# Second attention: a unit's last two batches of key tiles become one batch of four, with six buffers of exponentials

## What is computed

```python
mask = (q_idx >= k_idx) & (q_idx - k_idx <= WINDOW)      # WINDOW = 1024
scores = jnp.einsum('bhqd,bhkd->bhqk', q, k) / np.sqrt(HD)   # 16 heads of 32
attn = jax.nn.softmax(jnp.where(mask, scores, NEG), axis=-1)
out = jnp.einsum('bhqk,bhkd->bhqd', attn, v)
```

## Time and profile before

| | |
|---|---|
| median of 3 runs | 1531.86 us (1527.9 to 1532.23) |
| profiled execution, own time | 1528.64 us |
| its span, first to last instruction | 1526.9 us |
| mean granted TensorE clock | 0.984 |
| PE busy | 1463.1 us, 96% |
| DVE, ACT, POOL busy | 1027.9, 755.3, 464.2 us |
| S, line 2022 | 576 matmuls, 135.9 us |
| V, line 2059 | 1152 matmuls, 221.3 us |
| M, line 2000 | 592 matmuls, 179.0 us |

### The profile page before, as it was taken

The page is one execution under the profiler, slowest core; times in us unless marked ns, Lnnn a source line. Parts: engine busy times, 40 slices in busy tenths (PEclk is TensorE's granted clock), DMA queues, the critical chain, the costliest instruction groups (busy, mean ns, idle before and its releaser), DMA issues. The chain is left out here.

```text
span 1526.9 us, 23551 instructions
## 1 busy us (share of the span) xinstructions
PE 1463.1 (96%) x6981; PEld 1060.2 (69%) x6981; DVE 1027.9 (67%) x2940; ACT 755.3 (49%) x1282; POOL 464.2 (30%) x697
## 2 busy tenths in 40 slices
PE   6999999999999999999989999999999997998997
PEld 4778788888777888788855555555555554787776
DVE  6453666666658647887768886665668985678592
ACT  5633555656564535433325555555555553235561
POOL 0000577777620113323221212222212214053062
PEclk9999999999999999999969999999999999999999
DMA  5001222221100434466696405325145028743121
GB/s 187 1 1 45 108 90 76 86 103 76 56 29 26 146 102 121 138 195 192 191 241 281 112 16 121 71 59 122 28 100 121 6 81 259 208 173 138 31 81 14
DMA packets 106932, 161.53 MB, mean 106 GB/s; under 512 B 12640, under 2 KB 63728, under 8 KB 100432
## 3 DMA queue, kind: packets, MB, share of 16 engines
q1 hardware_dynamic: 101292, 152.53, 33.0%
q10 hardware_dynamic: 4516, 5.38, 1.0%
q0 software_dynamic: 1024, 2.43, 0.8%
HBM read 117.44 MB, written 42.87 MB: 105 GB/s over the span
## 5 line engine op out<-in xcount | busy, mean ns | idle before, releaser
L2147 ACT ACTIVATE l_pt<-banks 128x1024 f32<-128x1024 f32 (+3 forms) x288 | 218.6, 811 | 137.2 <-PE banks L2022 135.2
L2219 DVE CUSTOM_DVE_ANT_0 stage<-banks,l_edges 128x384 f32<-128x384 f32 (+3 forms) x384 | 201.8, 542 | 72.8 <-issue 71.5
L2059 PE MATMUL banks<-l_pt,l_v 128*64 128x512 f32 (+3 forms) x1152 | 221.3, 505 | 0.3 <-POOL l_pt L2117 0.3
L718 POOL TENSOR_TENSOR ex_hl<-ex_h,ex_hh 128x512 fp32r<-128x512 f32 x128 | 165.6, 1300 | 81.2 <-ACT ex_hh L686 81.0
L2116 POOL TENSOR_TENSOR l_turn<-l_before 128x2 f32<-128x2 f32 x192 | 38.9, 203 | 382.7 <-ACT l_pt L2147 373.3
L751 DVE SCALAR_TENSOR_TENSOR ex_rw<-banks,ex_wb 128x512 f32<-128x512 f32 x128 | 88.3, 691 | 78.9 <-PE banks L75 78.8
L2222 DVE TENSOR_REDUCE l_mx<-banks 128x1 f32<-128x384 f32 (+1 forms) x208 | 113.1, 544 | 39.8 <-PE banks L2000 39.0
L686 ACT ACTIVATE ex_hh<-ex_h 128x512 fp32r<-128x512 f32 x128 | 80.9, 632 | 103.5 <-DVE ex_h L759 102.0
L2059 PEld LDWEIGHTS banks<-l_pt,l_v 128*64 128x64 f32 x1152 | 69.1, 137 | 89.3 <-issue 67.8
L73 PE MATMUL banks<-ex_xlh,ex_wh 128*128 128x512 f32 x256 | 101.7, 397 | 2.0 <-DVE ex_rw L751 2.0
L74 PE MATMUL banks<-ex_xll,ex_wh 128*128 128x512 f32 x256 | 99.8, 390 | 0.0
(11 more groups left out here) (458 smaller groups left out, 3488.4 us busy)
## 6 DMA issues: line engine op xcount, KB each, us to landing
ex_wb<-gates_by_expert SPq DMA_DIRECT2D x16, 1024.0 KB, 4.7
l_v<-layer_v SPq DMA_DIRECT2D x8, 1024.0 KB, 17.2
layer_qk<-qkv_yh SPq DMA_DIRECT2D x30, 256.0 KB, 3.2
layer_qk<-qkv_yl SPq DMA_DIRECT2D x30, 256.0 KB, 3.6
layer_v<-qkv_vs SPq DMA_DIRECT2D x15, 512.0 KB, 4.6
ex_ws<-ew_in SPq DMA_DIRECT2D x16, 384.0 KB, 4.9
l_q<-layer_qk SPq DMA_DIRECT2D x12, 512.0 KB, 7.7
l_k<-layer_qk SPq DMA_DIRECT2D x12, 512.0 KB, 13.3
```

Of the source, the lines that this page charges most:

```text
L718: pool.tensor_tensor(hl[:, k % RING, :], h[:, k % RING, :], raw(hh[:, k % RING, :]), ALU.subtract).then_inc(hl_done, 1)
L2059: last = pe.matmul(bank[h * 2 * HD:(h + 1) * 2 * HD, (qa - b * BT) * P:(qz + 1 - b * BT) * P], v[par][:, kt, h, :], pt[:, step_part(b, j), ...
L2147: act.activation(pt[:, step_part(b, j), :, 0:width], G.banks[:, 2 * slot:2 * slot + 2, 0:width], ACT.Exp, scale=scale).then_inc(p_done, 1)
L2219: dve.tensor_tensor_reduce(cutoff[:, n % 4, 0:width], G.ps[5 + n % MB][:, 0:width], masked, 1.0, NEG, ALU.add, ALU.max, mx[:, h, m, c:c + ...
```

## The change

The last two batches of every unit become one batch of four key tiles (`BATCHES`). In such a batch at j the order of PE is: two places of the stream, S(j + 2), one place, S(j + 3), all the other places that the two batches had, S of the next unit's first two key tiles, then V of j, j + 1, j + 2 and j + 3 together. In the very last unit `picks` stands where the next unit's S would. Blocks 1 to 3 keep their batches of two before it; block 0, with four key tiles, is a batch of four alone. Batches of two keep their order.

Six buffers of exponentials replace four: four where they were, two in a new tile `far`. To make room, `junk` (a result of the ranking that nobody reads) has one half instead of two, and the one-hot tile moves to the place of the first value tile, free by then. ACT's first `output` also waits for the last writes of the stage before (`v_out`, `qk_out`).

```diff
-    PR = 4
+    PR, NEAR = 6, 4
+    BATCHES = [[4], [2, 2, 4], [2, 2, 2, 2, 4], [2, 2, 2, 2, 4]]
+        far = M.sb("far", [P, PR - NEAR, 2, TB])
...
-            return (keys_before[b] + j) % PR
+            n = (keys_before[b] + j) % PR
+            return pt[:, n, :, :] if n < NEAR else far[:, n - NEAR, :, :]
...
-                    for j in range(0, steps, 2):
-                        events = list(due(i, position(u, j + 1), last))
-                        ahead = min(MB, len(events)) if j + 2 < steps else len(events)
-                        for at in events[:ahead]:
-                            maximum(*at)
+                    for j, size in zip(accumulate([0] + BATCHES[b][:-1]), BATCHES[b]):
+                        events = [at for n in range(1, size, 2) for at in due(i, position(u, j + n), last)]
...
+                        else:
+                            for n, part in ((2, events[:2]), (3, events[2:MB])):
+                                for at in part:
+                                    maximum(*at)
+                                scores(i, u, j + n)
+                            for at in events[MB:]:
+                                maximum(*at)
+                            if end:
+                                picks()
+                            else:
+                                scores(i, u + 1, 0)
+                                scores(i, u + 1, 1)
+                        for n in range(size):
+                            values(i, u, j + n)
...
+                if not i_at_least(i, u, 1):
+                    for n in range(2):
+                        act.wait_ge(G.v_out[n], 16 * NT // 2)
+                        act.wait_ge(G.qk_out[n], 64 * NT // 2)
                 act.activation(ob[:, b % 2, :], G.ps[4], ACT.Copy).then_inc(o_sb, 1)
```

More of the change, by code:

```diff
@@ L11 @@
 from contextlib import ExitStack
+from itertools import accumulate
 import numpy as np
@@ L1793, in stage_attend1 @@
         "sr_in", "iota", "link", "sel", "pos_mm", "oh", "pick_mm"))
-    PR = 4
+    PR, NEAR = 6, 4
     LEAD = 37
-    PLACES, PICKS = 0, 8
+    BATCHES = [[4], [2, 2, 4], [2, 2, 2, 2, 4], [2, 2, 2, 2, 4]]
+    PLACES = 0
     MB = 3
@@ L1807, in stage_attend1 @@
         wraw = nc.alloc_sbuf_tensor_at("l1_wraw", [P, NC, D], F32, offset=v0_at)
-        pt = nc.alloc_sbuf_tensor_at("l1_pt", [P, PR, 2, TB], F32, offset=G.qw_at)
+        pt = nc.alloc_sbuf_tensor_at("l1_pt", [P, NEAR, 2, TB], F32, offset=G.qw_at)
         ob = M.sb("ob", [P, 2, TB])
         dn, dn2 = M.sb("dn", [P, 2 * H0 * TB // P]), M.sb("dn2", [P, H0 * TB // P])
-        sr, junk, same = G.out_o1[:, :, :].rearrange("p g n -> p (g n)"), M.sb("junk", [P, 2, T], BF16), M.sb("same", [P, 2, P])
+        sr, junk, same = G.out_o1[:, :, :].rearrange("p g n -> p (g n)"), M.sb("junk", [P, T], BF16), M.sb("same", [P, 2, P])
         count, rank_of, sel = M.sb("count", [P, NT, 6]), M.sb("rank", [P, NT]), M.sb("sel", [P, NT], BF16)
@@ L1814, in stage_attend1 @@
         order, before = M.sb("order", [P, SEL]), M.sb("before", [P, P])
-        onehot, number = junk[:, :, :].rearrange("p a (b n) -> p (a b) n", n=SEL), M.sb("number", [P, NT, 2], BF16)
+        onehot, number = nc.alloc_sbuf_tensor_at("l1_onehot", [P, NT, SEL], BF16, offset=v0_at), M.sb("number", [P, NT, 2], BF16)
         onesb, parti = M.sb("onesb", [P, P], BF16), M.sb("parti", [P, NT], I32)
@@ L2059, in values @@
                     last = pe.matmul(bank[h * 2 * HD:(h + 1) * 2 * HD, (qa - b * BT) * P:(qz + 1 - b * BT) * P],
-                                     v[par][:, kt, h, :], pt[:, step_part(b, j), h, 0:(qz - qa + 1) * P],
+                                     v[par][:, kt, h, :], step_part(b, j)[:, h, 0:(qz - qa + 1) * P],
                                      start=j == 0, stop=j == len(plans[b].keys) - 1)
@@ L2072, in body @@
                     end = last and u == 2 * NB - 1
-                    steps = len(plans[b].keys)
-                    for j in range(0, steps, 2):
-                        events = list(due(i, position(u, j + 1), last))
-                        ahead = min(MB, len(events)) if j + 2 < steps else len(events)
-                        for at in events[:ahead]:
-                            maximum(*at)
+                    assert sum(BATCHES[b]) == len(plans[b].keys)
+                    for j, size in zip(accumulate([0] + BATCHES[b][:-1]), BATCHES[b]):
+                        events = [at for n in range(1, size, 2) for at in due(i, position(u, j + n), last)]
                         if end and j == PLACES:
                             places()
[L2081 to L2091, removed]
+                        if size == 2:
+                            for at in events[:MB]:
+                                maximum(*at)
+                            scores(i, u, j + 2)
+                            scores(i, u, j + 3)
+                            for at in events[MB:]:
[3 more added lines that the diff above has]
+                                for at in part:
+                                    maximum(*at)
+                                scores(i, u, j + n)
+                            for at in events[MB:]:
+                                maximum(*at)
+                            if end:
[5 more added lines that the diff above has]
+                            values(i, u, j + n)
             looped(pe, PAIRS // 2, body)
@@ L2112, in masked @@
                 at, sign = (0, 1) if cut(b, j) == "diag" else ((qz - qa) * P, -1)
-                tile = pt[:, step_part(b, j), :, at:at + P]
+                tile = step_part(b, j)[:, :, at:at + P]
                 pool.wait_ge(p_done, keys + j + 1)
@@ L2146, in exponentials @@
                 wait(act, av_mm, n - PR + 1)
-                act.activation(pt[:, step_part(b, j), :, 0:width],
+                act.activation(step_part(b, j)[:, :, 0:width],
                                G.banks[:, 2 * slot:2 * slot + 2, 0:width], ACT.Exp, scale=scale).then_inc(p_done, 1)
@@ L2257, in rank @@
                     k0, k1 = pieces[n]
-                    dve.tensor_scalar(junk[:, t % 2, k0:k1], sr[:, k0:k1], own, 0.0, ALU.is_ge if k1 <= t * P else ALU.is_gt,
+                    dve.tensor_scalar(junk[:, k0:k1], sr[:, k0:k1], own, 0.0, ALU.is_ge if k1 <= t * P else ALU.is_gt,
                                       ALU.add, accum_out=count[:, t, n:n + 1])
```

## The result

The changed kernel takes 1543.29 us (median of 4 runs, 1540.88 to 1543.76) against 1532.05 us of the kernel before: 1.008 times as long, with a 95% interval of 1.0068 to 1.0092. The medians differ by 11.2 us. The forecast was 1545, between 1539 and 1552, and slower; the time lies inside. The profiled execution took 1543.76 us, against 1528.64 before: 15.1 us more, where the sum said 15. These two executions are further apart than the medians, since the one of before lies 3.4 us under its kernel's median and the one of after 0.5 above.

What follows compares the result with a forecast made beforehand. PE was taken to set the time, and merged batches to wait for banks held by DVE and ACT. Pairs' costs, saved V blocks included, summed to +15 us: 1545 forecast, range 1539 to 1552, 8 in 10 between 1534 and 1564.

Steps and rivals of the forecast that it cites:

- The bank rule: In merged batches, M needs a bank DVE has reduced, one each 0.475 us: place n + 3 not before 1.11 + 0.475 (n - 1).
- Block 0: Last batches' first place to next unit's first: from 6.04 to 6.53 us, +0.5, with PE waiting 1.2 us for banks.
- ACT's copies: Block 1's merged batch: seventh place waits for ACT's two copies until 2.91 us, next S until 3.5; stretch 6.83, +0.8.
- The V block's worth: One V block less in each of 32 units saves 0.35 us, between 0.155 and 0.465: -11.2 us in all.
- Block 3: Stretch with R second of five places: ACT's copies done at 1.94 us, S at 2.4, end at 4.8 against 4.23, +0.55.
- Block 2: Stretch with five narrow M and no R: 4.1 us against 3.97, +0.1.
- The first unit of the stage: Pair 0, block 0: three reductions no longer run under V0 and V1, +1.4 us, less 0.35 for the V block.
- Pair 7: Last pair, stream run out by blocks 2 and 3: 0.5, 0.8, 0 and -0.3 us for the four blocks, 1.0 together.
- What costs nothing: Six buffers, POOL's masks, ACT's `output` and new wait, `junk` and the one-hot tile add no time; `picks` within 0.4 us.
- rival 2: The clock also falls after the new waits, about 1.5 us a fall: 1557, or 1569 with blocks 0 and 1; chance 0.16.
- The sum: Whole program: pairs 1 to 6 11.7 us, pair 0 2.5, pair 7 1.0; +15 us on the profiled 1528.64, 1543.6.
- Rival 1: Drains go and no wait comes, if DVE returns a bank each 0.2 us, not 0.475: 1519 us; chance 0.10.

Runs made afterwards that it cites:

- e_short_after: The changed kernel with each of DVE's reductions cut to 128 columns of a bank: 1516.68 us, 0.9908 of the kernel before.
- e_buffers: All of the change but the batches of four, against the kernel before (six buffers, batches of two in the old order): 1531.25 us, ratio 1.0008.
- e_blocks01: The changed kernel with the batch of four in blocks 0 and 1 only, batches of two in blocks 2 and 3: 1544.75 us, 1.0102 of the kernel before.
- e_short_before: The kernel before with each of DVE's reductions cut to 128 columns of a bank: 1506.58 us, 0.9851 of the kernel before.
- LEAD = 41 and 44: Changed kernel, stream lead 41 or 44 for 37, stream places in batches of four split around the next unit's S: 1536.19 and 1535.61 us.

## Why the prediction was right

Most steps held and a few did not. The waits inside the merged batches are the ones that I named, in the places that I named.

- **The bank rule.** M behind the second narrow S spaced by 0.475: measured 0.47 to 0.49. V block of 4, 3, 2, 1 at 2.31: measured 2.30. Block 0 came out 0.09 above the forecast, block 2 0.04. e_short_after shows the cause, by taking it away.
- **ACT's copies.** Last bank at 2.91 behind the batch's start: the M released by them came 2.89 behind it (998.48 to 1001.37). The next unit's first S I had at 3.5, it came at 3.59, and S then took 1.12 (1002.07 to 1003.19) in place of 1.01: the first S after a wait takes 0.34 to the second, where 0.23 is usual. I had kept such a surcharge (0.1 for the weights behind each M that waited) for the upper bound, and should have put it into the sum wherever a wait stands right ahead. Block 3 (+0.70 for +0.55) has a like surplus, 0.06 ahead of S and 0.09 in it.
- **The V block's worth.** 0.35 (0.36 by its own terms), between 0.155 and 0.465. Where little wait is left, 0.27 (block 0, short reductions); with reductions of full length and spread places 0.18. The value taken was somewhat high; the rest of it, two thirds of M's and S's surplus (0.31), was an estimate, and about half of it is there.
- **Block 2** I had from pairs of odd number alone. In even ones the third narrow S of before starts 0.33 behind the second (953.41 to 953.74), twice the 0.16 between the first two; after the change an M stands between them (960.36), and the block gained 0.25.
- **The first unit of the stage.** Forecast +1.05, measured -1.06 (32.42 to 31.36 us), wrong in sign. I had three reductions lie under V0 and V1 and be lost. In fact V0 and V1, 3.1 us at the lower clock, stood ahead of R. PE waited for the copies of R, and nine more M came behind them, bound by DVE. After the change R comes 3.2 us earlier in the stage (20.2 behind its first M and not 23.4) and the V block last. Before, then after:

```profile
788.77 3.16 PE L2059 MATMUL banks<-l_pt,l_v 128*64 128x512 f32 x8
791.86 0.43 PE L2005 MATMUL banks<-identr,l_mrow 128*34 128x128 f32 x4
792.12 0.57 PE L2000 MATMUL banks<-k,q 96*128 96x384 f32 x2
793.57 0.79 PE L2000 MATMUL banks<-k,q 96*128 96x384 f32 x3 [0.88 <-ACT q L2166]
```

```profile
789.28 0.64 PE L2009 MATMUL banks<-identr,l_mrow 128*34 128x128 f32 x4
789.75 1.17 PE L2004 MATMUL banks<-k,q 96*128 96x384 f32 x2
791.21 4.44 PE L2004 MATMUL banks<-k,q 96*128 96x384 f32 x9 [0.28 <-ACT q L2181]
```

- **Pair 7** grew by 1.8 where I had 1.0. One of the five falls (at 1266.7) is in it.
- **What costs nothing.** For the buffers, `junk` and ACT's new wait e_buffers bears it out: 1.0008, an interval that holds 1. That POOL's masks and `output` are hidden in the merged batch was not tested by itself.
- **The clock (rival 2)** came true in part: four more falls than before, about 1.6 us each (1.5 forecast), some 6.5 us, less some 1.5 for the longer tail of before's first low clock (with a tail of 1.1 us in place of 4.5, e_buffers passes that unit in 14.76 us and not 16.29). I had said one in each unit of block 1 or none. So a third of the 15.1 us of this execution is the clock's, which my sum had at nothing.
- **The sum** hits the profiled time to 0.1 us, and that is partly luck. Against the medians it is 4 us too high (15 for 11.2), and terms missed on both sides: measured less forecast, in us, first unit -2.1, rest of pair 0 -0.7, pair 1 +2.9 (two falls), pairs 2, 3 and 5 +0.1, +0.4 and +0.45, pair 4 -1.2 (a fall more, but the wait and the fall at the loop's jump gone), pair 6 -0.4, pair 7 +0.8.
- **The page on the clock.** The Trainium skill (TensorE: Matmul & The Clock Gate, "A second HAM failure mode") tells of a kernel in which short idle times from cycling through PSUM banks made the clock swing. Here the trace agrees in part: three of the five falls begin in a merged batch with such waits, but most of the units with them stayed at the upper level, 1.00. What decides between the two stays open: the two stretches of e_blocks01 above have the same instructions of PE and nearly the same starts. No run here separates it.
- **Rival 1** was refuted on its own condition: DVE gave a bank back each 0.48, and once it did so faster (e_short_after), block 0 gained.

Open as well: where half of the 24 us of e_short_before lies, and what of the longer units of block 2 and 3 with LEAD = 41 and 44 is not the wait of R or a fall.

## What to carry to other kernels

A block of other work between two runs of a producer is not only a switch that costs something; it may be the time in which the consumer of a small ring of buffers catches up. Before merging, compare the length of the run with the number of buffers and the consumer's pace, not its average load, and ask of every in-order engine what it does between taking a buffer and giving it back (here 1.2 us of copies). If you merge, spread the run between the other groups in the same edit, then look at whole units and not only at the stretch you edited, since a wait that leaves one place tends to turn up in another.

## What the runs showed of the hardware

- One block of V less is worth 0.27 us to the unit (block 0, short reductions, 5.63 for 5.90), in V itself 0.16 (2.30 for 1.66 and 0.80).
- Short waits on a bank hide in PE's busy time: five M that start 0.2 apart where nothing holds them started 0.47 to 0.49 apart, and were shown as one row of 2.36 us without idle time. PE's busy time rose by 9.2 us with the same instructions, a part of it at the lower clock.
- The S behind a wait was followed by the next after 0.34 us in place of 0.23 (1002.07 to 1002.41, block 1 of after).
- A fall of the granted clock to 0.50 (1.2 GHz) lasted 3.4 us, in some cases 6.8, and one of 3.4 cost 1.6. With the same instructions it came in one unit and not in another: block 0 of e_blocks01 8.19 and 6.62. Waits of 0.86 in seven pairs of e_short_after brought none.
- DVE at two thirds of busy time still costs PE at 96% some 24 us: halving its reductions (0.55 to 0.29) made the kernel before 1.5% faster.
